# A trajectory blend with a routed expert network on one core: scales from sums of squares, a gate that carries the factor, one z operation, weights by chunk

## The chip, the cores and the metric

The kernel runs on one core of a Trainium2 chip. The metric is the time of one execution on the device, in microseconds; the kernel before has a median of 218.2 us over three runs (217.67 to 218.41). All work is one launch; five engines (TensorE, VectorE, ScalarE, GpSimd, and SyncE, which starts transfers) run their own instruction lists and wait for each other by semaphores.

## What is computed

The input is 16 sequences of 256 tokens with 128 features (4096 tokens). First a guided trajectory over a window of eight differences is added and normalized; then each token goes through one of eight experts, chosen by the router, and is normalized again.

```python
diffs = x[:, 1:] - x[:, :-1];  windows = the last 8 diffs at each position
mag = norm(windows);  normed = windows / mag;  combined = pos_weights * tanh(2 * mag)
g_weights = softmax(2 * cos(normed, guidance));  influence = g_weights @ guidance
traj = sum((0.6 * normed + 0.4 * influence) * combined) / sum(combined)
x = layernorm(x + traj)                                     # x1
logits = x @ Wr + br;  gates = max(softmax(logits));  e = argmax(logits)
xn = layernorm(x) * ln_g + ln_b
h = relu(xn @ W1[e] + b1[e]);  y = (h @ W2[e] + b2[e]) * gates      # 128 -> 512 -> 128
x = layernorm(x + y)
```

## The kernel before

**Stage 1** handles the tokens in eight parts (index u) of 512 tokens, as four tiles of 128. It is pipelined by hand: an outer iteration i, from -2 to 11, holds on each engine the pieces of several parts, in a fixed order. On VectorE it is `window(i)` (L706: the step v = i - 1 that makes V from the influence, the step y = i - 2 that makes Y = x + traj and its statistics, the routing steps r = i - 3 and g = i - 4, all interleaved with `drain`s), then `diff(i + 2)` (the differences Dd), `factors` (reciprocal magnitudes of part i + 1, the bias term of x1 of part i - 2), and `directions(i + 1)` (the normalized N). On ScalarE it is nT (copy of the transposed N), weights_hi from i = 7 on, ET (the exponential, L586), ex, tanh of part i + 1, x1 of part i - 2 (L593), four squares with sums of part i + 2 (L559), xT, V of part i + 1 (L573). On TensorE it is the transpose of N, logits of part i - 3 (L445), similarities of part i (L454), traj of part i - 1 (L433), rank of part i - 3, influence of part i (L406), transpose of x1 of part i - 2. On GpSimd it is the root of the squares (L340), the two roots of the variance (L345, L349) and, from i = 4, `scatter(i - 4)`: four indirect DMAs (L357) that write each token's row of 132 values (x1, gate, second root, token number) to a table in HBM sorted by expert.

**Scales.** TensorE multiplies in fp16 with weights and activations split into a high and a low part, each scaled by a power of two. The scales come from maxima of the absolute values: VectorE's `maxima1` (W1, L844, after `directions` in i = 0 and 1) and `maxima2` (W2, L849, and the small ones, before `directions` in i = 2 to 4), a transpose and a product on TensorE in i = 5, and ten `scales` steps in window 6. Then ScalarE writes the high parts of the weights (L611, L612, two experts at a time) in i = 7 to 10 and VectorE the low parts (L909, L911) in i = 7, in i = 9, and twice behind the table of blocks. The biases are split into three parts by ScalarE (L635, L638, L639) and VectorE (L901 in i = 8, L904 in i = 9).

**Between the stages** VectorE makes the table of blocks (which rows and which expert each of the 39 blocks of 128 rows has), SyncE waits for all scatters and TensorE for the low parts of the weights.

**Stage 2** runs over 39 blocks, again as a pipeline in a fixed order per engine, written with `steps([(lead, function), ...])`: in step b a function with lead d handles block b + d. SyncE loads a row tile XR (L303), eight buffers. ScalarE: xs (L649, lead 5), hh (L663, lead 1), OUT (L672, lead -3), xt (L654, lead 4), sd (L668, lead -2), xh (L658, lead 4). TensorE: h (L526 to L530, lead 1), the transpose of xs (L501, lead 4), the next eight expert numbers into registers (L511, every eighth step), y (L540 to L543, lead 0; hh times 256 columns of W2hl, which holds high and low part side by side, then hl times the high part). VectorE: hl (L986, lead 1), mv (L1005, lead -1), zpart (L991, lead 0), the reciprocal (L1009, lead -2), z (L995, lead 0), the shift (L1013, lead -2), bn (L999, lead 0), xl (L980, lead 4). GpSimd: the store of OUT by token number (L388, lead -3), then cg, the gate times the inverse scale, and a copy of the token number (L381, L382, lead 3).

Of the kernel before, what the change touches and what calls it, by code (L numbers as in the profile page):

```python
# [41 lines left out]
UN = 8  # L42
LN_EPS = 1e-5
# [37 lines left out]
def build(nc, x, guide, wr, br, ln_g, ln_b, w1, b1, w2, b2, cst, rows, out):  # L81
    with ExitStack() as ctx:
# [3 lines left out]
        def sem(name):  # L86
# [22 lines left out]
        W1h = sb("W1h", [P, E, FF], F16)  # L109
        W1l = sb("W1l", [P, E, FF], F16)  # L110
        W2hl = sb("W2hl", [P, E, FC, 2 * D], F16)
# [4 lines left out]
        mx = sb("mx", [P, 16])  # L116
        mx4 = sb("mx4", [4, 8])
# [49 lines left out]

        XR = [sb(f"XR{i}", [P, ROW]) for i in range(UN)]
        tok = [sb(f"tok{i}", [P, 1], I32) for i in range(UN)]
        xs = [sb(f"xs{i}", [P, D]) for i in range(UN)]  # L170
        cg = [sb(f"cg{i}", [P, 1]) for i in range(UN)]
# [5 lines left out]
        z0 = [sb(f"zpart{i}", [P, D]) for i in range(UN)]  # L177
# [3 lines left out]
        sd = [sb(f"sd{i}", [P, 3]) for i in range(UN)]  # L181
# [3 lines left out]
        ld = {n: sem("ld_" + n) for n in ("cst", "guide", "small", "x0", "x1", "x2", "x3", "w1", "w2", "bias")}  # L185
# [3 lines left out]
                 "counted guide_sq guide_norm guided guideT_ps guideT split_hi split_lo maxima maxT_ps max4 maxb_ps max_read scales_w "  # L189
# [5 lines left out]
        names2 = "xs xh xl hl z".split()  # L195
        t = {n: [sem(f"b_{n}{i}") for i in range(UN)] for n in names2}

        every = {n: sem("every_" + n) for n in "token xT_ps xt h_ps hh y_ps z0 bn mv sd rec shift out".split()}
        seen = sem("seen")
        row_loaded = [sem(f"row_loaded{i}") for i in range(UN)]  # L200
# [5 lines left out]
        infl_ps, traj_ps, xT_ps, log_ps = [bank[2], bank[3]], [bank[4], bank[5]], bank[6], bank[7]  # L206
        rank_ps = bank[5][:, 300:300 + NT * E]
# [13 lines left out]

        LO_AT = (7, 9)
# [28 lines left out]
        def _(sp):  # L251
# [14 lines left out]
            for n, (a, b) in enumerate(((2, 6), (6, 10), (10, 16)), 1):  # L266
                sp.dma_start(X[:, a:b, :, :], x[a:b].rearrange("b (p c) d -> p b c d", c=2)).then_inc(ld[f"x{n}"], 16)
                next_rows(a, b, f"x{n}")
                if n == 1:
                    sp.dma_start(W1[:, :, :], w1.rearrange("e d f -> d e f")).then_inc(ld["w1"], 16)  # L270
            sp.dma_start(Wr[:, :], wr).then_inc(ld["small"], 16)
            sp.dma_start(brb[:, :], br.rearrange("(a e) -> a e", a=1).to_broadcast([P, E])).then_inc(ld["small"], 16)
            sp.dma_start(gb[:, 0:1], ln_g.rearrange("(d a) -> d a", a=1)).then_inc(ld["small"], 16)
            sp.dma_start(gb[:, 1:2], ln_b.rearrange("(d a) -> d a", a=1)).then_inc(ld["small"], 16)
            sp.dma_start(W2[:, :, :, :], w2.rearrange("e (c p) d -> p e c d", p=P)).then_inc(ld["w2"], 16)
            sp.wait_ge(s["zeroed"], 1)
            for j in range(3):
                sp.dma_start(bias[32 * j:32 * j + E, 0:FF], b1).then_inc(ld["bias"], 16)
                sp.dma_start(bias[32 * j:32 * j + E, FF:FF + D], b2).then_inc(ld["bias"], 16)
# [20 lines left out]
            def load(count, k):  # L300
                after(sp, every["z0"], blocks(count(-1), k))
                after(sp, every["token"], blocks(count(-1), k))
                sp.dma_start(XR[k][:, :], rows[bass.ds(row[count(0) * UN + k], P), :]).then_inc(row_loaded[k], 16)  # L303

            load_rows(0)
            for b in range(NB):
                if b % UN == UN // 2 and b + UN // 2 < NB:
                    load_rows(b + UN // 2)
                load(lambda d, turn=b // UN: turn + d, b % UN)
# [4 lines left out]
        def _(pool):  # L314
# [4 lines left out]
            pool.memset(mx[:, :], 0.0)  # L319
# [31 lines left out]

            def scatter(u):
                pool.wait_ge(s["placed"], u + 1)
                pool.wait_ge(s["x1"], u + 1)
# [12 lines left out]
            for i in range(-1, NU + 4):  # L367
                if i + 1 < NU:
                    mag_roots(i + 1)
                if 2 <= i <= NU + 1:  # L370
# [4 lines left out]
            def token(count, k):  # L375
                pool.wait_ge(row_loaded[k], count(1) * 16)
                pool.nop().then_inc(seen, 1)
                after(pool, stored[k], count(0) * 16)
                pool.nop().then_inc(seen, 1)

                pool.tensor_scalar(cg[k][:, :], XR[k][:, D:D + 1], scl[:, 3:4], None, ALU.mult)  # L381
                pool.tensor_copy(tok[k][:, :], XR[k][:, D + 2:D + 3].bitcast(I32)).then_inc(every["token"], 1)  # L382

            def store(count, k):
                pool.wait_ge(every["token"], blocks(count(0), k))
                pool.wait_ge(every["out"], blocks(count(0), k))
                pool.nop().then_inc(seen, 1)
                pool.indirect_dma_start(  # L388
                    out=out[:, :], out_offset=bass.IndirectOffsetOnAxis(ap=tok[k][:, 0:1], axis=0),
                    in_=OUT[k][:, :], in_offset=None, bounds_check=T - 1, oob_is_err=False).then_inc(stored[k], 16)  # L390

            steps([(-3, store), (3, token)])

        @block.tensor
        def _(pe):
# [13 lines left out]
            def xT_(u):  # L409
# [3 lines left out]
                if u == 3:  # L413
                    pe.wait_ge(s["max_read"], 1)
# [22 lines left out]
            def logits(u):  # L437
                pe.wait_ge(s["xT_sb"], u + 1)
                if u == 0:
                    pe.wait_ge(s["guideT"], 1)  # L440
                    pe.wait_ge(ld["small"], 64)
                if u >= 1:
                    pe.wait_ge(s["shifted"], u)
                for k in range(NT):
# [22 lines left out]
            for i in range(0, NU + 3):  # L467
                if i == 5:

                    pe.wait_ge(s["maxima"], 1)  # L470
                    pe.wait_ge(s["xT_sb"], 3)
                    pe.transpose(xT_ps[0:4, 0:P], mx[:, 0:4], ident).then_inc(s["maxT_ps"], 1)
# [564 lines left out]
```

## Time and profile before

| | |
|---|---|
| median of three runs | 218.2 us (217.67 to 218.41) |
| the profiled execution | 218.13 us, span 216.3 us |
| mean granted TensorE clock | 0.811 of 2.4 GHz |
| busy: TensorE, VectorE, ScalarE, GpSimd | 150.0, 171.1, 141.6, 122.3 us |
| stage 1: first load to last scatter | 0.7 to 120.5 us |
| stage 2: first row load to last store's start | 123.0 to 209.3 us |

The profile page comes from one execution by the hardware profiler, times in microseconds from the start of the span. A row of a timeline gives start, duration, engine, line of the kernel, operation, output and inputs, and in brackets how long the engine stood idle before it and what released it; "issue" is time in which it waited for nothing that the profile shows. A duration includes the latency of the operation; neighbours on an engine overlap a little, so the distance from start to start is what an operation costs on a full engine. The granted clock is a share of 2.4 GHz: 0.50 is 1.2 GHz, 1.00 is 2.4 GHz. PE is TensorE, DVE VectorE, ACT ScalarE, POOL GpSimd, SP SyncE; PEld is the load of TensorE's stationary operand.

### The profile page before, as it was taken

How to read it: one execution, taken by the hardware profiler on the slowest of the kernel's cores; microseconds unless marked ns; L12 is line 12 of the kernel's file. 1: busy time of each engine (PE TensorE's matmuls, PEld its weight loads, DVE VectorE, ACT ScalarE, POOL GpSimd, SP SyncE). 2: the span in 40 equal slices, each digit the busy share in tenths (PEclk: the TensorE clock that was granted, in tenths of full speed). 3: DMA queues.
4: the chain of work that ended last, by engine and by line, in shares of the span. 5: the costliest groups of instructions: out<-in, count | busy, mean ns of one | idle time of the engine just before them, and what ended most of it. 6: DMA issues, size and time to landing. Idle time of an engine off the chain costs nothing.

```text
span 216.3 us, 5485 instructions
## 1 busy us (share of the span) xinstructions
PE 150.0 (69%) x1395; PEld 125.7 (58%) x1395; DVE 171.1 (79%) x792; ACT 141.6 (65%) x425; POOL 122.3 (57%) x210
## 2 busy tenths in 40 slices
PE   0057974998777898674510069999899999899600
PEld 0015753685756487573400059899798898788400
DVE  2447789878998988986868517999999999999910
ACT  2357627483835567737712078999999999998530
POOL 4322213423728775877877240377777787678670
PEclk9999997575888597855555558999999999999955
DMA  5996770000100100001015140222222222220000
GB/s 147 355 364 193 213 200 0 3 0 2 39 13 22 34 25 25 27 28 50 25 52 150 36 89 16 50 66 60 70 74 77 71 64 70 75 64 23 31 10 2
DMA packets 16417, 15.76 MB, mean 73 GB/s; under 512 B 2810, under 2 KB 13142, under 8 KB 16386
## 3 DMA queue, kind: packets, MB, share of 16 engines
q1 hardware_dynamic: 13458, 10.83, 18.3%
q0 software_dynamic: 2272, 4.27, 6.0%
q10 hardware_dynamic: 656, 0.30, 0.5%
q8 instruction: 13, 0.21, 0.4%
q14 instruction: 18, 0.15, 0.2%
HBM read 10.52 MB, written 5.33 MB: 73 GB/s over the span
## 4 chain that ended last, share of the span: by engine, by line
PE 21%; ACT 20%; POOL 18%; DVE 15%; issue 13%; DMA 5%; DVEq 2%; SPq 1%; ACTq 1%; POOLq 1%
POOL rows L357 12%; ACT OUT L672 4%; PE bank L433 3%; PE bank L540 3%; DMA XN<-in_attn_embeddings 3%; ACT xs L649 3%; DVE hl L986 3%; ACT xt L654 3%; PE bank L454 3%; POOL rstd L345 2%; POOL R L349 2%; ACT sq L559 2%; ACT hh L663 2%; PE bank L526 2%; PE bank L528 2%
## 5 line engine op out<-in xcount | busy, mean ns | idle before, releaser
L388 POOL DMA_INDIRECT out<-OUT,tok x39 | 40.4, 1037 | 25.1 <-issue 23.9
L357 POOL DMA_INDIRECT rows<-R,place x32 | 34.0, 1061 | 9.0 <-issue 9.0
L526 PE MATMUL bank<-sel,bias 96*128 96x128 bf16 x156 | 35.2, 226 | 0.0
L540 PE MATMUL bank<-W2hl,hh 128*128 x156 | 32.6, 274 | 3.5 <-issue 2.6
L528 PE MATMUL bank<-xh,W1h 128*128 128x128 f16 x156 | 34.9, 224 | 0.0
L530 PE MATMUL bank<-xh,W1l 128*128 128x128 f16 x156 | 34.7, 223 | 0.0
L529 PE MATMUL bank<-xl,W1h 128*128 128x128 f16 x156 | 34.7, 222 | 0.0
L433 PEld LDWEIGHTS bank<-V,C 128*128 128x128 f32 x128 | 24.9, 299 | 11.2 <-issue 11.2
L986 DVE SCALAR_TENSOR_TENSOR hl<-bank,hh 128x512 f16<-128x512 f32 x39 | 26.9, 690 | 3.0 <-ACT hh L663 2.8
L433 PE MATMUL bank<-V,C 128*128 128x129 f32 x128 | 26.8, 393 | 3.0 <-DVE Y L753 3.0
L543 PE MATMUL bank<-W2hl,hl 128*128 x156 | 27.9, 219 | 0.0
L663 ACT ACTIVATE hh<-bank 128x512 f16<-128x512 f32 x39 | 23.4, 599 | 3.2 <-PE bank L530 2.7
L501 PE MATMUL bank<-C,xs 128*128 128x128 f32 x39 | 11.7, 300 | 14.0 <-ACT xs L649 14.0
L672 ACT ACTIVATE OUT<-z,sd 128x128 f32<-128x128 f32 x39 | 19.6, 502 | 2.5 <-DVE sd L1013 2.5
L649 ACT ACTIVATE xs<-XR 128x128 f32<-128x128 f32 x39 | 15.9, 408 | 7.9 <-DMA XR<-rows 7.6
L540 PEld LDWEIGHTS bank<-W2hl,hh 128*128 128x128 f16 x156 | 15.2, 98 | 8.7 <-issue 7.0
L345 POOL TENSOR_TENSOR rstd<-var_in,minus_half 128x4 f32<-128x4 f32 x8 | 8.2, 1020 | 20.0 <-DVE var_in L784 20.0
L654 ACT ACTIVATE xt<-bank,gbs 128x128 f32<-128x128 f32 x39 | 18.0, 462 | 0.0
L454 PE MATMUL bank<-nT,gdT 128*64 128x512 f32 x16 | 13.1, 911 | 5.0 <-ACT nT L580 5.0
L381 POOL TENSOR_SCALAR cg<-XR,scl 128x1 f32<-128x1 f32 x39 | 12.0, 309 | 7.3 <-DMA XR<-rows 5.5
L528 PEld LDWEIGHTS bank<-xh,W1h 128*128 x156 | 15.8, 101 | 0.1
L526 PEld LDWEIGHTS bank<-sel,bias 96*128 96x128 bf16 x156 | 15.5, 99 | 0.4
(161 smaller groups left out, 448.9 us busy)
## 6 DMA issues: line engine op xcount, KB each, us to landing
XR<-rows SPq DMA_DIRECT2D x39, 66.0 KB, 2.0
W<-in_ffn_W SPq DMA_DIRECT2D x1, 2048.0 KB, 11.3
X<-in_attn_embeddings SPq DMA_DIRECT2D x2, 512.0 KB, 9.0
X<-in_attn_embeddings SPq DMA_DIRECT2D x1, 768.0 KB
out<-OUT,tok POOLq DMA_INDIRECT x39
XN<-in_attn_embeddings SPq DMA_DIRECT2D x2, 256.0 KB, 8.2
rows<-R,place POOLq DMA_INDIRECT x32, 2.4
C<-in_constants SPq DMA_DIRECT2D x1, 428.0 KB, 5.2
```

Of the source, the lines that this page charges most:

```text
L357: pool.indirect_dma_start(out=rows[:, :], out_offset=bass.IndirectOffsetOnAxis(ap=place[u % 4][:, k:k + 1], axis=0), in_=R[u % 4][:, k, :] ...
L388: pool.indirect_dma_start(out=out[:, :], out_offset=bass.IndirectOffsetOnAxis(ap=tok[k][:, 0:1], axis=0), in_=OUT[k][:, :], in_offset=None ...
L433: m = pe.matmul(tile_of(traj_ps, k), band[a][k % 2], V[u % 3][:, 2 * (k // 2) + a, :], start=a == 0, stop=a == 1)
L526: pe.matmul(h, bias3[:, c * P:(c + 1) * P], sel, start=True, stop=False)
L528: pe.matmul(h, wh, xh[k][:, :], start=False, stop=False)
L529: pe.matmul(h, wh, xl[k][:, :], start=False, stop=False)
L530: m = pe.matmul(h, wl, xh[k][:, :], start=False, stop=True)
L540: pe.matmul(y[:, 0:2 * D], hh[k][:, c * P:(c + 1) * P], w, start=c == 0, stop=False)
L543: m = pe.matmul(y[:, 0:D], hl[k][:, c * P:(c + 1) * P], wh, start=False, stop=c == FC - 1)
L663: act.activation(hh[k][:, :], bank[1 + k % 4][:, :], ACT.Relu).then_inc(every["hh"], 1)
L672: act.activation(OUT[k][:, :], z[k][:, :], ACT.Identity, scale=sd[k][:, 1:2], bias=sd[k][:, 2:3]).then_inc(every["out"], 1)
L986: stt(hl[k][:, :], bank[1 + k % 4][:, :], 0.0, hh[k][:, :], ALU.max, ALU.subtract).then_inc(t["hl"][k], 1)
```

## The change

Five parts.

1. The scales come from sums of squares in place of maxima. ScalarE squares W1 (i = 0, 1), the small tensors (i = 2) and W2 (i = 2, 3) with an accumulated sum, between nT and ET; one matmul on TensorE in i = 3, ahead of infl, sums over the partitions; the steps stand in window 4 (the last ones behind its last cast, each behind a drain), with one more root on GpSimd. The loads of the biases, the gains and W2 move ahead in SyncE's list.
2. The inverse of the scales is multiplied into the gate in stage 1 (`gated`, on VectorE, which the scatter waits for), so that stage 2 needs no cg; the store reads the token number from the row tile itself. Row tiles get 16 buffers, and a load of block b waits for the store of block b - 16.
3. y is accumulated in 128 columns, the low part of W2 added in the same place: one z operation.
4. The last scaling moves from ScalarE (OUT, lead -3) to VectorE (`b_fin`, lead -2), as (z - mean) * reciprocal; the shift goes.
5. The weights are split by chunks of 128 of the 512 middle features, in separate tiles; the high parts are written in i = 5 to 8, the bias parts in i = 5 to 7.

```diff
             for n, (a, b) in enumerate(((2, 6), (6, 10), (10, 16)), 1):
                 sp.dma_start(X[:, a:b, :, :], ...)
                 next_rows(a, b, f"x{n}")
                 if n == 1:
                     sp.dma_start(W1[:, :, :], w1.rearrange("e d f -> d e f")).then_inc(ld["w1"], 16)
+                    sp.wait_ge(s["zeroed"], 1)
+                    (six bias loads, two of the gains)
+                if n == 2:
+                    sp.dma_start(W2[:, :, :, :], w2.rearrange("e (c p) d -> p e c d", p=P)).then_inc(ld["w2"], 16)
...
-            steps([(-3, store), (3, token)])
+            steps([(0, store)])
...
+                if i == 3:
+                    pe.wait_ge(s["sums"], 6)
+                    pe.wait_ge(s["gains"], 1)
+                    pe.wait_ge(s["shifted"], 1)
+                    pe.matmul(sums_ps, ones[:, :], sums[:, :], start=True, stop=True).then_inc(s["sums_ps"], 1)
...
+                pe.matmul(y[:, 0:D], sel16[...], bias3[:, FF:FF + D], start=True, stop=False)
                 for c in range(FC):
-                    pe.matmul(y[:, 0:2 * D], hh[k][:, c * P:(c + 1) * P], w, start=c == 0, stop=False)
-                    m = pe.matmul(y[:, 0:D], hl[k][:, c * P:(c + 1) * P], wh, start=False, stop=c == FC - 1)
+                    pe.matmul(y[:, 0:D], hh[k][:, c * P:(c + 1) * P], wh, start=False, stop=False)
+                    pe.matmul(y[:, 0:D], hl[k][:, c * P:(c + 1) * P], wh, start=False, stop=False)
+                    m = pe.matmul(y[:, 0:D], hh[k][:, c * P:(c + 1) * P], wl, start=False, stop=c == FC - 1)
...
+            def squares_w1(q):
+                if q == 0:
+                    act.wait_ge(ld["w1"], 16)
+                act.activation(junk[:, :], W1[:, 2 * q:2 * q + 2, :], ACT.Square, accum_out=sums[:, 8 + q:9 + q])
+                act.drain()
...
                 if 0 <= i < NU:
                     nT_(i)
-                if i >= NU - 1:
-                    weights_hi(i - NU + 1)
+                if 0 <= i < 2:
+                    squares_w1(2 * i)
+                    squares_w1(2 * i + 1)
+                if i == 2:
+                    squares_bias()
+                if 2 <= i < 4:
+                    squares_w2(2 * i - 4)
+                    squares_w2(2 * i - 3)
+                if i in HI_AT:
+                    weights_hi(HI_AT.index(i))
                 if 0 <= i < NU:
                     et(i)
...
-            steps([(5, b_xs), (1, b_hh), (-3, b_fin), (4, b_xt), (-2, b_sd), (4, b_xh)])
+            steps([(5, b_xs), (1, b_hh), (4, b_xt), (-2, b_sd), (4, b_xh)])
...
+            def gated(g):
+                if g >= 4:
+                    dve.wait_ge(scattered[g % 4], 16 * NT * (g // 4))
+                ts(R[g % 4][:, :, D], gate[:, :], scl[:, 3:4], None, ALU.mult).then_inc(s["gated"], 1)
...
                     dve.tensor_copy(oh16[:, :, :], oh[:, :, :]).then_inc(s["onehot"], 1)
-                if i == 6:
-                    scales(9)
+                if i == 4:
+                    scales(6)
+                    for step in range(7, 11):
+                        dve.drain()
+                        scales(step)
+                    dve.drain()
+                    gated(0)
...
-                if 8 <= i <= 9:
-                    split_bias(i - 8)
+                if 6 <= i <= 7:
+                    split_bias(i - 6)
...
-            steps([(1, b_hl), (-1, b_mv), (0, b_z0), (-2, b_rec), (0, b_z), (-2, b_shift), (0, b_bn), (4, b_xl)])
+            steps([(1, b_hl), (-1, b_mv), (0, b_z), (-2, b_rec), (0, b_bn), (-2, b_fin), (4, b_xl)])
```

## Rows read from the trace of the kernel before

**Rows 1.** Chain of work that ended last: start, duration, what

```profile
119.57 2.34 DMA rows<-R,place
```

**Rows 2.** Timeline of GpSimd, a scatter of part 5

```profile
104.02 2.00 POOL L357 DMA_INDIRECT rows<-R,place  x1 [0.18 <-issue]
```

**Rows 3.** Timeline of VectorE in stage 1

```profile
46.70 0.24 DVE L727 RECIPROCAL st<-bank 128x2 f32<-128x2 f32 x2 [1.01 <-PE bank L406]
...
95.02 0.81 DVE L901 TENSOR_TENSOR bias_r<-bias 96x640 f32<-96x640 f32 x1
...
100.55 0.19 DVE L771 TENSOR_TENSOR lg<-bank,brb 128x32 f32<-128x32 f32 x1 [1.39 <-PE bank L445]
...
109.74 0.19 DVE L808 TENSOR_TENSOR oh<-oh,rt 128x32 f32<-128x32 f32 x1
110.00 0.18 DVE L813 CAST oh<-oh 128x32 bf16<-128x32 f32 x1
```

**Rows 4.** Busy time by stretch: PE, PEld, DVE, ACT, POOL, granted clock, DMA

```profile
42.00:44.00 2.00, 2.00 (x11) 2.00 (x11) 1.92 (x6) 1.25 (x6) 0.83 (x2) 0.50 0.04 8
...
150.00:170.00 20.00, 18.89 (x266) 17.14 (x265) 19.67 (x86) 19.75 (x64) 15.40 (x31) 1.00 0.26 70
```

**Rows 5.** Timeline of VectorE in stage 2

```profile
129.94 0.69 DVE L986 SCALAR_TENSOR_TENSOR hl<-bank,hh 128x512 f16<-128x512 f32 x1 [0.97 <-ACT hh L663]
...
166.35 0.69 DVE L986 SCALAR_TENSOR_TENSOR hl<-bank,hh 128x512 f16<-128x512 f32 x1
...
167.04 0.32 DVE L991 SCALAR_TENSOR_TENSOR zpart<-bank,cg,XR 128x128 f32<-128x128 f32 x1
167.28 0.15 DVE L1009 RECIPROCAL sd<-sd 128x1 f32<-128x1 f32 x1
...
167.66 0.15 DVE L1013 SCALAR_TENSOR_TENSOR sd<-mv,sd 128x1 f32<-128x1 f32 x1
167.78 0.29 DVE L999 BATCH_NORM_STATS2 bn<-z 128x6 f32<-128x128 f32 x1
...
168.24 0.69 DVE L986 SCALAR_TENSOR_TENSOR hl<-bank,hh 128x512 f16<-128x512 f32 x1
```

**Rows 6.** Timeline of TensorE in stage 2: transposes, and a y

```profile
132.77 0.28 PE L501 MATMUL bank<-C,xs 128*128 128x128 f32 x1
...
134.52 0.28 PE L501 MATMUL bank<-C,xs 128*128 128x128 f32 x1
...
185.22 0.28 PE L540 MATMUL bank<-W2hl,hh 128*128 x1 [0.91 <-issue]
```

**Rows 7.** Timeline at the end: last hl, last store

```profile
202.58 0.69 DVE L986 SCALAR_TENSOR_TENSOR hl<-bank,hh 128x512 f16<-128x512 f32 x1
...
209.25 0.97 POOL L388 DMA_INDIRECT out<-OUT,tok  x1 [0.30 <-issue]
```

**Rows 8.** Groups of instructions by line and shape: busy, mean ns, idle before

```profile
L672 ACT ACTIVATE OUT<-z,sd 128x128 f32<-128x128 f32 x39 | 19.6, 502 | 2.5 <-DVE sd L1013 2.5
...
L836 DVE TENSOR_SCALAR N<-Dd,st 128x128 f32<-128x128 f32 x32 | 7.1, 286 | 0.7
...
L559 ACT ACTIVATION_READ_ACCUMULATOR sq<-Dd 128x1 f32 x32 | 6.0, 187 | 0.0
...
L849 DVE TENSOR_REDUCE mx<-W 128x1 f32<-128x1024 f32 x4 | 4.8, 1210 | 0.0
...
L611 ACT ACTIVATE W1h<-W,scl 128x1024 f16<-128x1024 f32 x4 | 4.6, 1140 | 0.0
```

**Rows 9.** Timeline of ScalarE, the exponential of part 0

```profile
16.15 0.59 ACT L586 ACTIVATE ET<-bank 64x512 f32<-64x512 f32 x1 [2.06 <-PE bank L454]
```

**Rows 10.** Page, part 6, DMA issues: KB each, us to landing

```profile
W<-in_ffn_W SPq DMA_DIRECT2D x1, 2048.0 KB, 11.3
```

**Rows 11.** Timeline of TensorE in stage 1, traj of parts 1 and 2

```profile
29.95 2.02 PE L433 MATMUL bank<-V,C 128*128 128x129 f32 x16 [0.61 <-DVE Y L753]
...
41.41 3.81 PE L433 MATMUL bank<-V,C 128*128 128x129 f32 x16
```

More of the change, by code:

```diff
@@ L42 @@
 UN = 8
+RN = 16
 LN_EPS = 1e-5
@@ L193, in build @@
         padded = sem("padded")
-        names2 = "xs xh xl hl z".split()
+        names2 = "xs xh xl hl".split()
         t = {n: [sem(f"b_{n}{i}") for i in range(UN)] for n in names2}
-        every = {n: sem("every_" + n) for n in "token xT_ps xt h_ps hh y_ps z0 bn mv sd rec shift out".split()}
+        every = {n: sem("every_" + n) for n in "xT_ps xt h_ps hh y_ps z bn mv sd rec out".split()}
         seen = sem("seen")
-        row_loaded = [sem(f"row_loaded{i}") for i in range(UN)]
+        row_loaded = [sem(f"row_loaded{i}") for i in range(RN)]
         stored = [sem(f"stored{i}") for i in range(UN)]
@@ L298, in load_rows, with load @@
                     row[first + j] = sp.snap(held_row[half + j], min_val=0, max_val=PADROW)
[L300 to L303, printed above, removed]
+            def load(b):
+                if b >= RN:
+                    sp.wait_ge(stored[b % UN], 16 * ((b - RN) // UN + 1))
+                sp.dma_start(XR[b % RN][:, :], rows[bass.ds(row[b], P), :]).then_inc(row_loaded[b % RN], 16)
             load_rows(0)
@@ L467, in _ @@
             for i in range(0, NU + 3):
[L468 to L472, printed above, removed]
                 if i < NU:
@@ L478, in _ @@
                     sims(i)
-                if i == 5:
-                    pe.wait_ge(s["max4"], 1)
-                    pe.matmul(xT_ps[:, P:P + 4], ones[0:4, :], mx4[:, 0:4], start=True, stop=True).then_inc(s["maxb_ps"], 1)
                 if 1 <= i <= NU:
@@ L660, in b_hh @@
             def b_hh(count, k):
-                act.wait_ge(every["token"], blocks(count(0), k))
                 act.wait_ge(every["h_ps"], blocks(count(0), k))
@@ L665, in b_sd @@
             def b_sd(count, k):
-                after(act, stored[k], count(0) * 16)
                 act.wait_ge(every["mv"], blocks(count(0), k))
                 act.activation(sd[k][:, 0:1], mv2[k][:, 1:2], ACT.Sqrt, bias=epsc[:, 0:1]).then_inc(every["sd"], 1)
-            def b_fin(count, k):
-                act.wait_ge(every["shift"], blocks(count(0), k))
-                act.activation(OUT[k][:, :], z[k][:, :], ACT.Identity, scale=sd[k][:, 1:2], bias=sd[k][:, 2:3]).then_inc(every["out"], 1)
-            steps([(5, b_xs), (1, b_hh), (-3, b_fin), (4, b_xt), (-2, b_sd), (4, b_xh)])
+            steps([(5, b_xs), (1, b_hh), (4, b_xt), (-2, b_sd), (4, b_xh)])
         @block.vector
@@ L861, in power, with gain_sums @@
-            def power(dst, src, k, second):
-                if second:
-                    return ts(dst.bitcast(I32), dst.bitcast(I32), -1.0, float((254 + k) << 23), ALU.mult, ALU.add)
-                return ts(dst.bitcast(I32), src.bitcast(I32), POW2_MASK, None, ALU.bitwise_and)
+            def gain_sums():
+                dve.wait_ge(s["sums"], 4)
+                ts(sums[:, 0:4], sums[:, 8:12], sums[:, 13:14], None, ALU.mult).then_inc(s["gains"], 1)
+            QX, QH, Q2, Q1 = range(4)
```

243 lines of the change are left out of this document (114 added, 129 removed).

## The prediction, made before the changed kernel was run

> **What bounds the kernel now.** I read the busy times by stretch first, then the chain of work that ended last, then the timelines of single engines. The kernel has two stages with different limits. Stage 1 ends when the last scattered row has landed: the last landing begins at 119.57 us [rows 1], and only then are block rows fetched. That chain runs along GpSimd: twelve scatters, of parts 5, 6 and 7, follow each other without a wait from 104.02 us [rows 2], about 1.27 us from start to start. What set 104.02 is the root of part 7, which waits for VectorE's variance, which stands behind a wait of 1.39 us for the logits of part 6 [rows 3], which come through ScalarE and TensorE from the root of part 6. So before 104 us GpSimd, VectorE and ScalarE hand one chain around; what any of them adds there shifts the end.
> In stage 2, VectorE is busy 19.67 and ScalarE 19.75 of 20 us, TensorE 18.89 [rows 4]. VectorE starts hl every 1.89 us (166.35, 168.24) [rows 5]. TensorE needs less where it waits for nobody: 1.75 us from transpose to transpose (132.77, 134.52) [rows 6]. So VectorE and ScalarE bound a block and TensorE is 0.14 us behind them. From the first hl (129.94) [rows 5] to the last (202.58) [rows 7] there are 38 intervals in 72.64 us, 1.91 each.
>
> **Stage 2, part by part.** VectorE loses the first of two z operations: 0.24 us from its start to the next (167.04 to 167.28), and the shift, 0.12 (167.66 to 167.78) [rows 5]. It gains the last scaling, a tensor_scalar of 128x128 with two pointer scalars; its nearest row is L836, 0.286 us alone [rows 8], about 0.22 where four follow each other (my reading: 0.88 for four). 1.89 - 0.24 - 0.12 + 0.22 = 1.75, or 1.81 if the whole 0.286 shows. ScalarE loses OUT, 0.50 alone [rows 8], at least 0.38 between neighbours: about 1.50, free. GpSimd loses two small operations and keeps the store; it was not the bound. TensorE's y goes from four matmuls of 256 columns and five of 128 to thirteen of 128: the columns are the same, four more instructions cost about 0.01 in all: 1.76. So the bound passes to TensorE, with VectorE level with it.
> Now its stalls count. Every eight blocks the sequencer loads expert numbers and TensorE stands 0.6 to 1.1 us (0.91 at 185.22) [rows 6]; four such stalls. Before, VectorE didn't notice them. Behind a TensorE without slack each costs its whole length, about 0.75. Floor: 38 x 1.76 + 4 x 0.75 = 69.9; with some jitter between two equal engines 70.3. Against 72.64 that is 2.3 us less (bounds: 3.3 less if half of the stalls hide, 0.8 less if VectorE needs 1.81 and the stalls are not caught up).
> The fill of stage 2 is limited by landing rows and the first matmuls, which the change leaves: zero (if sixteen early fetches crowd the first four, up to +0.5).
> The end: last hl at 202.58, last store started at 209.25 [rows 7], 6.67 us. The stores of the last four blocks stand 1.27 apart on GpSimd. The scaling now comes one block earlier in the order than OUT did, so the last store is bound by GpSimd: the store of the fourth block from the end can start 1.6 us after the last hl, three more follow at 1.27, 5.4 us: 1.2 us less (0 to 2.0).
>
> **Stage 1, part by part.** Removed from VectorE: eight maxima of 1.21 us [rows 8], of which the four of W1 lay behind waits at 17 to 26 us, and some 1.2 us of smaller ones and waits; the scales of window 6, about 1.65 with the two bias scalings. Added to ScalarE: eight squares. The nearest row is L611, 1.14 us for the same shape, plus 0.187 for reading the accumulator [rows 8], less an overlap of 0.1 and plus a drain: 1.3 each, 2.6 per iteration, ahead of the exponentials (L586) of iterations 0 to 3.
> The Trainium skill (ScalarE: Activation LUTs, What ACT_TABLE_LOAD costs) gives 186 ns + 0.833 ns per element for an ACTIVATE with an immediate scale: 1.04 us for a square, by an estimate from that page. By that the two squares would be 0.2 us shorter; the sum keeps the row.
> Iteration 0: ScalarE waited 2.06 us for the similarities before L586 at 16.15 [rows 9]. W1 lands at about 14.1 to 14.6 (issued at 3.3, 11.3 to landing) [rows 10], so two squares end at 16.7 to 17.2 and L586 comes 0.6 to 1.05 late. Everything behind it on ScalarE (tanh, squares of the next part, V, nT) is on the chain there: +0.6 to +1.05 from then on. In iterations 1 to 3 the squares delay L586 by 1.6 to 3.4 us, which traj on TensorE mostly hides: it took 3.81 us at 41.41 [rows 11], at 1.2 GHz (granted 0.50 in that stretch) [rows 4]. The cover is thin: infl comes about 0.2 us later still, with the new matmul ahead of it, and VectorE waited for infl already (1.01 us at 46.70) [rows 3]. So window 4 starts its V about 1.2 to 1.6 us late, and the maxima removed from iterations 2 and 3 bring nothing, since what follows waits for TensorE.
> Iteration 4 holds the scales. Inside the window they add about 0.7; behind the last cast come gbs, four more steps and the gate's product, with drains. A drain with one small operation takes 0.26 (109.74 to 110.00) [rows 3]; five of these, the two bias scalings (0.75) and gbs make 2.4. So the differences of part 6 and the bias term of part 2's x1 come some 4.3 us late, while directions, in front of which 3.55 us of maxima vanish, come 0.8 late. ScalarE then runs x1, four squares, xT, V and nT of the next part in that order: nT of part 5 is 4 us late, similarities and traj follow, and infl of part 5 is 2 to 3 us late; VectorE had about 1.3 us before it needed that. At window 6 the delay is 1 to 2 us; its removed scales (1.65) bring it to about +0.5 at its end, but the split of the bias (0.81 at 95.02) [rows 3] moved there takes it back, and infl of part 6 (bias copy on ScalarE, 0.72, ahead of nT) holds window 7 at +1.5. In iteration 7 the second bias piece, 0.82, moves in front of window 8. Before, both stood where VectorE waited for logits anyway (the 1.39) [rows 3]. The root of part 6 is then 2.0 to 2.4 late, and that delay goes on to the last scatter one to one.
> Queues passed. SP: six bias and two gain loads stand ahead of x[6:10] and W2 ahead of x[10:16]; both were needed late (22 us and 42 us), some 7 MB have come by then at the 330 to 400 GB/s of the first slices: zero, at most +1. GpSimd: the root of the weights (1.02) waits for window 4's third step and lies under the wait for the variance of part 2; the first scatter, which waits for the gate, is 3.4 us late, behind it the root of part 6, but GpSimd stood idle 4.2 us before the next variance: absorbed. The weights' high parts move from iterations 7 to 10 to 5 to 8, under waits of ScalarE; the low parts stay, two of four behind the table, and end about 0.9 us before the rows land: hidden.
> Sum of stage 1: +1.9 (between -1.5, if TensorE runs at 2.4 GHz where it had 1.2 and the squares hide, and +4.5).
>
> **Sum.** The profiled execution has 218.13 us, of which 216.3 is span; 0.07 under the median of 218.2. 218.13 + 1.9 - 2.3 - 1.2 = 216.5.
>
> **A rule against the change.** In stage 1 one scatter took 2.00 us against 0.96, at 104.02 [rows 2], while VectorE split weights (two SBUF inputs). A store in stage 2 takes 1.05 and 0.36 of issue, 1.41 of 1.76. If the new scaling on VectorE held it as long as that scatter was held, GpSimd would need 2.4 per block and 38 blocks would take 91 us: 238. If it is held only for the 0.286 of the scaling, 1.69 stays under 1.76. The Trainium skill (Advanced Engine Details and Errata, VectorE Performance Modes) says that VectorE's second SBUF port is shared with GpSimd and that two-port instructions block it, which a fp32 tensor_scalar in SBUF can be; by that rule, the trace agrees for the splits.
>
> **The rivals.**
> A (the forecast, 0.42): stage 1 later by about 1.9, stage 2 shorter by 3.5.
> B, stage 1 doesn't shift (0.25): the squares hide fully and fewer stalls keep TensorE at 2.4 GHz, where traj takes 2.02 (29.95) instead of 3.81 [rows 11]. For it: VectorE loses some 6.8 us of work in iterations 2 to 5 and it is busy nearly throughout. Against: in iterations 3 and 4 TensorE's own work fills the period. 218.1 - 0.3 - 3.5 = 214.3.
> C, slower (0.19): the chain diff, x1, squares, xT, V, nT behind window 4 finds TensorE at 1.2 GHz, and the two bias splits add; similarities (1 us more) and traj (1.8 more) then lie on the path. It decides once infl of part 5 is more than 3.5 us late. Stage 1 +4.7, stage 2 -3.0: 219.8.
> D, no change (0.12): TensorE's stalls and VectorE at 1.81 leave 0.8 in stage 2, the end 0.9, stage 1 +1.9: 218.3.
> E, GpSimd becomes the bound of stage 2 (0.02): 238, above.
>
> **How the numbers follow.** About 0.3% (0.65 us) is what a measurement can tell from no change: faster is below 217.5, slower above 218.9. A lies mostly below 217.5 (0.34 of 0.42, the rest within), B below; C and E above; D within, a third of it above. Faster 0.59, same 0.16, slower 0.25. The likeliest time is A's 216.5. The range 213.2 to 220.2 takes in B and most of C; A's own range is 215.0 to 218.0.
>
> **What would show it.** Right: OUT is gone from ScalarE and it idles about 0.3 us per block; TensorE goes from transpose to transpose in 1.76 to 1.80; hl first to last about 70.3; last hl to last store 5.4; L586 of part 0 near 17 us; the last scatter starts near 121.5. Wrong: a last scatter before 119 (then B), after 123 (then C); hl intervals at 1.85 or more between the stalls; a store longer than 1.3 us; a ScalarE wait for W1 or W2.

## The result, and the profile after

The changed kernel takes 226.5 us (median of four runs, 226.04 to 226.72) against 218.3 us for the kernel before beside it (217.67 to 220.16): a ratio of 1.036, with a 95% interval of 1.029 to 1.042. The profiled execution took 226.56 us with a span of 224.3, against 218.13 and 216.3. So it is 8 us slower where 1.7 us faster was forecast, and outside the range of 213.2 to 220.2. Of the some 10 us between forecast and result, 7.7 arose in stage 2, 1.2 in stage 1 and 0.9 at the end.

The span divides at four points that both traces have. All times are us.

| | before | after | difference | forecast |
|---|---|---|---|---|
| last scatter starts | 119.57 | 122.66 | +3.1 | +1.9 |
| from there to the first hl | 10.37 | 10.23 | -0.1 | 0 |
| first to last hl, 38 intervals | 72.64 | 78.01 | +5.4 | -2.3 |
| last hl to last store | 6.67 | 6.35 | -0.3 | -1.2 |

The ends of these stretches in the trace of after, from the timelines of GpSimd and VectorE (start, duration, engine, line, operation, and in brackets how long the engine stood idle before it and what released it), to be held against [rows 2, 5, 7]:

```profile
122.66 0.96 POOL L368 DMA_INDIRECT rows<-R,place  x1 [0.30 <-issue]
...
132.89 0.69 DVE L992 SCALAR_TENSOR_TENSOR hl<-bank,hh 128x512 f16<-128x512 f32 x1 [0.91 <-ACT hh L697]
...
210.90 0.69 DVE L992 SCALAR_TENSOR_TENSOR hl<-bank,hh 128x512 f16<-128x512 f32 x1 [0.36 <-ACT hh L697]
...
217.25 0.98 POOL L393 DMA_INDIRECT out<-OUT,XR  x1 [0.31 <-issue]
```

Stage 2 is where most of it went. Busy times of after in 150 to 170 us (busy us and number of instructions of TensorE, its weight loads, VectorE, ScalarE, GpSimd; granted clock, DMA share, GB/s), the counterpart of [rows 4]:

```profile
150.00:170.00 20.00, 19.45 (x296) 17.93 (x296) 17.66 (x69) 15.74 (x50) 9.58 (x10) 1.00 0.23 59
```

VectorE has gone from 19.67 to 17.66 and ScalarE from 19.75 to 15.74, so both have the room that the change was to give them (a part of it only because the blocks are longer). What they wait for stands in the list of waits of after (us in total, times, longest):

```profile
POOL out L393 <- DVE OUT L1017: 53.7, 35, 17.6
ACT hh L697 <- PE bank L532: 19.2, 39, 1.7
DVE hl L992 <- ACT hh L697: 8.5, 25, 0.9
```

The shares of the chain that ended last, by engine, in the page of after (TensorE had 21% before):

```profile
PE 49%; ACT 12%; DVE 12%; DMA 7%; issue 7%; POOL 4%; DVEq 3%; ACTq 1%; SPq 1%; POOLq 1%
```

In stage 2 the waits lead to TensorE: GpSimd waits for VectorE, VectorE for ScalarE, ScalarE for TensorE, and from 140 to 200 us no wait of TensorE for one of them is listed. A piece of its timeline shows what it does in y:

```profile
162.94 0.22 PE L540 MATMUL bank<-bias,sel 96*128 96x128 bf16 x1
163.00 0.22 PE L543 MATMUL bank<-W2h,hh 128*128 x1
163.06 0.22 PE L544 MATMUL bank<-W2h,hl 128*128 x1
163.12 0.22 PE L545 MATMUL bank<-W2l,hh 128*128 x1
163.17 0.22 PE L543 MATMUL bank<-W2h,hh 128*128 x1
163.23 0.22 PE L544 MATMUL bank<-W2h,hl 128*128 x1
163.28 0.22 PE L545 MATMUL bank<-W2l,hh 128*128 x1
163.49 0.22 PE L543 MATMUL bank<-W2h,hh 128*128 x1
163.54 0.22 PE L544 MATMUL bank<-W2h,hl 128*128 x1
163.60 0.22 PE L545 MATMUL bank<-W2l,hh 128*128 x1
163.71 0.22 PE L543 MATMUL bank<-W2h,hh 128*128 x1
```

The matmuls follow each other in 0.05 to 0.06 us, but twice, ahead of L543, the next one starts 0.21 and 0.11 us after the matmul before it. A distance of 0.21 between starts is hidden by the 0.22 of duration, so no idle time is shown. From hl to hl it is 1.95 us now (median of the 38 intervals), 1.89 before. The instructions that stand in these places are not matmuls. The view of one line names them, with count, shortest, middle and longest duration in ns (PEldq is TensorE's sequencer). The high parts of y in after:

```profile
L543 PEldq ALU_OP  x156: 32/32/32, 133.6 to 212.4; - x156
```

The low parts of y in after, the same view:

```profile
L545 PEldq ALU_OP  x156: 32/32/32, 133.7 to 212.5; - x156
```

And y in the kernel before, the same view:

```profile
L540 PEldq FUSED_REGOPS  x156: 46/46/46, 130.7 to 203.8; - x156
```

Each different start of a weight slice that depends on the expert's number costs one computation of an address. The kernel before needs four per block in y, since the high part begins where the pair of both does; the changed one needs eight. h has eight in both. So a block has 12 before and 16 after.

The 32 ns of such a row are not what it costs. The starts of these rows in the trace of after show it: behind an ALU_OP the next address computation never begins sooner than 0.112 us, behind a FUSED_REGOPS never sooner than 0.124, with the matmuls and weight loads handed out in between. Without the pauses of more than 0.25 us they stand 0.120 apart on average. Sixteen of them make 1.92 of the 1.95 us of a block; twelve at that distance would make 1.44, less than the 1.75 that TensorE and VectorE need.

In stage 1 ScalarE does stand for W1, which was forecast as a sign of trouble:

```profile
15.44 1.06 ACT L613 ACTIVATE junk<-W 128x1024 bf16<-128x1024 f32 x1 [1.67 <-DMA W<-in_ffn_W]
16.40 0.18 ACT L613 ACTIVATION_READ_ACCUMULATOR junk<-W 128x1 f32 x1
16.66 1.06 ACT L613 ACTIVATE junk<-W 128x1024 bf16<-128x1024 f32 x1
17.62 0.19 ACT L613 ACTIVATION_READ_ACCUMULATOR junk<-W 128x1 f32 x1
17.90 0.59 ACT L588 ACTIVATE ET<-bank 64x512 f32<-64x512 f32 x1
```

The first exponential is 1.75 us late against [rows 9].

### The profile page after: what moved, and what is told of

Same layout as the page of the kernel before. It is cut to its first block, busy times and chain, and to the rows that moved or that the text cites. A ratio compares the mean times of both kernels' runs of the same rounds, so it can differ in the third digit from the quotient of the medians.

```text
span 224.3 us, 5683 instructions
## 1 busy us (share of the span) xinstructions
PE 153.5 (68%) x1550; PEld 129.1 (58%) x1550; DVE 158.7 (71%) x749; ACT 138.7 (62%) x405; POOL 104.6 (47%) x133
## 4 chain that ended last, share of the span: by engine, by line
PE 49%; ACT 12%; DVE 12%; DMA 7%; issue 7%; POOL 4%; DVEq 3%; ACTq 1%; SPq 1%; POOLq 1%
PE bank L543 6%; DMA W<-in_ffn_W 5%; PE bank L436 5%; PE bank L530 5%; PE bank L532 4%; PE bank L528 4%; PE bank L545 4%; PE bank L531 4%; PE bank L544 4%; PE bank L450 3%; POOL rows L368 3%; ACT R L595 3%; PE bank L459 3%; PE bank L503 2%; ACT sq L561 2%
## 5 line engine op out<-in xcount | busy, mean ns | idle before, releaser
L393 POOL DMA_INDIRECT out<-OUT,XR x39 | 38.3, 983 | 56.3 <-DVE OUT L1017 53.7
L545 PE MATMUL bank<-W2l,hh 128*128 x156 | 32.1, 218 | 0.0
L543 PE MATMUL bank<-W2h,hh 128*128 x156 | 31.8, 218 | 0.0
L544 PE MATMUL bank<-W2h,hl 128*128 x156 | 31.8, 218 | 0.0
L436 PEld LDWEIGHTS bank<-V,C 128*128 128x128 f32 x128 | 22.0, 267 | 10.5 <-issue 10.5
L436 PE MATMUL bank<-V,C 128*128 128x129 f32 x128 | 23.9, 361 | 1.5 <-DVE Y L785 1.5
L684 ACT ACTIVATE xs<-XR 128x128 f32<-128x128 f32 x39 | 15.3, 393 | 7.6 <-DMA XR<-rows 7.5
L689 ACT ACTIVATE xt<-bank,gbs 128x128 f32<-128x128 f32 x39 | 17.6, 452 | 0.1
L543 PEld LDWEIGHTS bank<-W2h,hh 128*128 128x128 f16 x156 | 15.1, 97 | 2.3
L532 PEld LDWEIGHTS bank<-xh,W1l 128*128 x156 | 15.3, 98 | 0.7
L531 PEld LDWEIGHTS bank<-xl,W1h 128*128 x156 | 15.6, 100 | 0.0
L528 PEld LDWEIGHTS bank<-sel,bias 96*128 96x128 bf16 x156 | 15.4, 99 | 0.0
```

What stands on the lines that cost most here:

```text
L393: pool.indirect_dma_start(out=out[:, :], out_offset=bass.IndirectOffsetOnAxis(ap=XR[b % RN][:, D + 2:D + 3].bitcast(I32), axis=0), in_=OUT ...
L436: m = pe.matmul(tile_of(traj_ps, k), band[a][k % 2], V[u % 3][:, 2 * (k // 2) + a, :], start=a == 0, stop=a == 1)
L528: pe.matmul(h, bias3[:, c * P:(c + 1) * P], sel, start=True, stop=False)
L531: pe.matmul(h, wh, xl[k][:, :], start=False, stop=False)
L532: m = pe.matmul(h, wl, xh[k][:, :], start=False, stop=True)
L543: pe.matmul(y[:, 0:D], hh[k][:, c * P:(c + 1) * P], wh, start=False, stop=False)
```

## The experiments

**Stage 2: what holds TensorE.** Theory Q: its queue can't deliver a block's matmuls, weight loads and address computations in 1.75 us. (The expectations call an address computation a register operation.) Four kernels were run together on one chip. In all four the trace shows something that neither kernel's had: 31 to 42 of some 176 signals of TensorE were seen 0.1 to 1.5 us after the matmul that sends them, also in stage 1, where three of the four kernels are the changed one but for the shape of a weight tile. One such place, from the timeline of wide_y (start, duration, engine, line, operation, idle time before it): TensorE's h ended at 153.50, and ScalarE, which waits for it alone, went on at 154.85.

```profile
153.28 0.22 PE L531 MATMUL bank<-xh,W1l 128*128 128x128 f16 x1
...
154.85 0.60 ACT L697 ACTIVATE hh<-bank 128x512 f16<-128x512 f32 x1 [1.44 <-PE bank L531]
```

Their times carry this, so I ran them again beside a control, on other chips. None of the other traces has one late signal in these bounds.

wide_y (y as before, z unchanged):

```diff
-                    pe.matmul(y[:, 0:D], hh..., wh, start=False, stop=False)
-                    pe.matmul(y[:, 0:D], hl..., wh, start=False, stop=False)
-                    m = pe.matmul(y[:, 0:D], hh..., wl, start=False, stop=c == FC - 1)
+                    w, wh = W2hl[c][:, bass.ds(e, 1), :], W2hl[c][:, bass.ds(e, 1), 0:D]
+                    pe.matmul(y[:, 0:2 * D], hh..., w, start=c == 0, stop=False)
+                    m = pe.matmul(y[:, 0:D], hl..., wh, start=False, stop=c == FC - 1)
```

> The changed kernel with TensorE's y as before (four matmuls of 256 columns, the low part of W2 beside the high one in each chunk's tile), VectorE's one z operation kept: it reads the first 128 columns, so the product of hh with the low part of W2 is left out of the result. Theory Q (TensorE's instruction queue can't deliver the instructions of a block in time: 30 matmuls with their weight loads and 16 register operations, 0.53 us of them; about 0.047 us per matmul and load): 26 matmuls and 12 register operations are 1.6 us, the queue is no bound, blocks return to 1.76 us between the expert loads, and the time is 218.5 to 219.5. Rival V (VectorE's operations or the row tiles' waits make the block 2.05 long, TensorE only follows): 226.

Measured 229.95 us, 1.052 of before [1.047, 1.057], with the late signals.

one_address (in y `wh = wl = W2h[c][:, bass.ds(e, 1), :]`):

> The changed kernel, with y's third matmul reading the high part of W2 again in place of the low one (so the low part is left out and the high one counted twice): the same 29 matmuls, but four register operations of 32 ns fewer per block. Theory Q: the queue needs 1.81 to 1.84 per block, 38 blocks gain 4 to 5 us: about 222. Rival N (the number of matmuls alone counts, register operations run beside them): 226.

Measured 229.05, with the late signals. fixed_expert (all slices `[:, 0:1, :]`, the weights of expert 0 for every block):

> The changed kernel with the weights of expert 0 for every block, so that no address is computed on TensorE (the choice of the expert's weights is left out; the numbers of the experts are still loaded). Theory Q: the queue needs 1.4 per block, TensorE's and VectorE's 1.75 are the bound: 217.5 to 219. Rival N (matmuls alone): 226.

Measured 227.42, with the late signals. before_narrow_y (for c > 0 the matmul of 256 columns is two of 128):

> The kernel before with three of its four matmuls of 256 columns in y cut into two of 128 (same columns, same results in the same places; three matmuls and three register operations more per block), nothing else changed. Theory Q: 29 matmuls and 15 register operations, 0.63 us of them, need 1.95 to 2.0 per block against 1.89: 221 to 223. Rival V (the block's length comes from VectorE or ScalarE): 218.3.

Measured 224.88. Taken alone, the first three would have thrown theory Q over. The control:

> The changed kernel itself, unchanged, as a control on the chip of this call: in the runs wide_y, one_address and fixed_expert the profile shows signals of TensorE that reached ScalarE 0.4 to 1.3 us after the matmul, in stage 1 too, where their instructions are those of the changed kernel. Theory C (that comes with the chip or its state): this run shows them too and is slower than the first runs of the changed kernel, 228 to 232. Rival K (it comes with the kernels): 226.5, and signals at most 0.03 us late.

Measured 226.87, 1.036 of before [1.028, 1.045], no late signals. The changed kernel is at its 226.5 here, and the repeats below have no late signals either, with the same instructions. So they belong to the chip or its state of the first four runs, and the rival that puts them on the kernels is out.

> The run wide_y again, beside the control (the product of hh with the low part of W2 is left out of the result). Theory Q (TensorE's instruction queue bounds the changed kernel's block): 5 to 7.5 us under after_again. Rival L (blocks shorter than about 1.9 us are not to be had for another reason): within 2 us of after_again or above it.

> The run fixed_expert again, beside the control (all blocks take the weights of expert 0, no address is computed). Theory Q: 5 to 8 us under after_again. Rival L: within 2 us of it or above.

Measured: wide_y_again 217.46, 9.4 us under the control; fixed_expert_again 216.10, 10.8 under it. Both speak for theory Q and against rival L, but both gain more than Q's range allowed (5 to 7.5, and 5 to 8). Neither is a usable kernel: wide_y_again leaves a product out, fixed_expert_again the choice of the expert. Starts of TensorE's transpose in wide_y_again, 1.75 and 1.74 apart:

```profile
149.74 0.28 PE L502 MATMUL bank<-C,xs 128*128 128x128 f32 x1
...
151.49 0.28 PE L502 MATMUL bank<-C,xs 128*128 128x128 f32 x1
...
153.23 0.28 PE L502 MATMUL bank<-C,xs 128*128 128x128 f32 x1
```

Which of the two differences counts, four matmuls or four addresses?

> The run one_address again, on another chip (y's third matmul reads the high part of W2 in place of the low one, which is left out; four register operations fewer per block, the same matmuls). In the control of the second call blocks follow each other in 1.95 us between the expert loads; with all 16 register operations gone 1.75. Theory Q (a matmul with its load costs the queue about 0.047 us, a register operation 0.032 to 0.046, and they add up): 1.82, stage 2 shorter by 5 to 6: 220.5 to 221.5. Rival N (the count of matmuls alone): 226.

Measured 217.73, 0.999 of before [0.996, 1.002]. With all 29 matmuls and four address computations fewer, the block is back at 1.75, and first to last hl takes 69.09 us. That is more than Q forecast (1.82 per block, 220.5 to 221.5 us): it took the 32 ns of a row for the whole cost. By the distances of 0.12 above, four computations fewer put the sequencer at 1.44, so another bound takes over. The count of matmuls doesn't make the 1.95; rival N is out. It is not nothing, though: the 29 matmuls and the transpose now start 0.055 to 0.06 us apart all through a block (0.115 behind the transpose), and that is 1.75. That this run reads one weight tile less in y is not the reason either, since fixed_expert_again reads all of them and has the same 1.75. Busy times of it in the same 20 us show VectorE full again:

```profile
150.00:170.00 20.00, 19.50 (x330) 19.03 (x328) 19.54 (x78) 17.98 (x57) 10.79 (x11) 1.00 0.28 75
```

The other direction, on the kernel before:

> The run before_narrow_y again, on another chip (the kernel before, three of y's four wide matmuls cut in two). Theory Q: 28 matmuls, a transpose and 15 register operations (0.63 us) make 2.0 per block against 1.89: 221.5 to 223.5. Rival V (VectorE and ScalarE set the block): 218.2.

Measured 223.69, 1.027 of before [1.023, 1.030]; the median interval between hl is 1.95 and the sum 77.91, as in the changed kernel. That is just above the forecast of 221.5 to 223.5. Stage 1 is untouched (last scatter at 119.60). So most of TensorE's part of the change (three of its four wide matmuls), put alone into the kernel before, makes it slower by some 5.7 us.

And the vector part alone, before_light:

```diff
-            steps([(1, b_hl), (-1, b_mv), (0, b_z0), (-2, b_rec), (0, b_z), (-2, b_shift), (0, b_bn), (4, b_xl)])
+            steps([(1, b_hl), (-1, b_mv), (0, b_z0), (-2, b_rec), (0, b_bn), (-2, b_fin), (4, b_xl)])
```

> The kernel before with the vector part of the change alone: one z operation (it reads the first 128 columns of y; the product of hh with the low part of W2 is left out of the result) and the last scaling on VectorE in place of ScalarE, no shift. TensorE, GpSimd, the row loads, the weights' tiles and stage 1 stay. Theory Q: blocks of 1.75 to 1.78 between the expert loads, stage 2 shorter by 2 to 2.5, the end by 0.3: 215 to 216. Rival L: 217.5 to 220.

Measured 214.92, 0.987 of before [0.979, 0.994], just under the forecast. First to last hl takes 69.70. But it leaves out a product, so it is no replacement.

| kernel | matmuls in h and y | addresses | median interval of hl | 38 intervals |
|---|---|---|---|---|
| before | 25 | 12 | 1.89 | 72.64 |
| after | 29 | 16 | 1.95 | 78.01 |
| before_narrow_y_again | 28 | 15 | 1.95 | 77.91 |
| one_address_again | 29 | 12 | 1.75 | 69.09 |
| wide_y_again | 25 | 12 | 1.74 | 69.25 |
| fixed_expert_again | 29 | 0 | 1.75 | 66.67 |

The last row has one thing more than its expectation says. The expert numbers are not loaded there: its trace has no instruction on the line of these loads, where the changed kernel has five (the view of that line, durations in ns):

```profile
L511 PEldq TENSOR_LOAD <-blk_e x5: 593/607/1069, 125.3 to 191.1; - x5
```

So fixed_expert_again drops sixteen addresses and four loads at once, and its long intervals are gone with the loads (at most 2.01, where wide_y_again has up to 2.72 and the changed kernel 3.29). It can't tell what a load costs beside no addresses. The other rows can: the four intervals behind the loads exceed the median by 0.8 to 1.3 us each in the changed kernel, and by 0.3 to 1.0 in one_address_again and wide_y_again, with twelve addresses.

**A version with the whole result.** light_alt keeps y and both z of before, takes the last scaling of every second block from ScalarE to GpSimd and the gate's factor from GpSimd to ScalarE, and has 16 row tiles:

> A kernel with the whole result: the kernel before with the row tiles in 16 buffers, the store's index read from the row tile, the gate's factor multiplied on ScalarE, and the last scaling of even blocks on GpSimd, of odd ones on ScalarE (with their shift); y and both z operations as before. Theory Q: TensorE's queue as before (1.73 at most), VectorE 1.83, ScalarE about 1.8, GpSimd about 1.5: blocks of 1.83, and the expert loads show in part: 215.5 to 217. Rival G (GpSimd's scaling is slow or is held up by VectorE and stores come late): 218 or more.

Measured 225.54, 1.035 of before [1.030, 1.041]: rival G. The median interval is 1.86 (72.43 for 38), but GpSimd falls behind, and the last store starts 14.66 us after the last hl. Its timeline at the end:

```profile
206.14 0.97 POOL L394 DMA_INDIRECT out<-OUT,XR  x1 [0.30 <-issue]
207.15 0.80 POOL L386 TENSOR_SCALAR OUT<-z,mv,sd 128x128 f32<-128x128 f32 x1
208.85 1.06 POOL L394 DMA_INDIRECT out<-OUT,XR  x1 [0.90 <-POOL OUT L386]
210.22 0.98 POOL L394 DMA_INDIRECT out<-OUT,XR  x1 [0.30 <-issue]
211.24 0.80 POOL L386 TENSOR_SCALAR OUT<-z,mv,sd 128x128 f32<-128x128 f32 x1
```

A scaling costs 0.80 on GpSimd, and its store another 0.90 until it starts: 4.1 us for two blocks, where two blocks of the kernel before take 3.8. I found no whole version that beats the kernel before.

**Stage 1: where 3.1 us come from.** First the three suspects together, all_three (the moved scale steps in words):

```diff
-                if 0 <= i < 2:
-                    squares_w1(2 * i)
-                    squares_w1(2 * i + 1)
+                if 1 <= i < 3:
+                    squares_w1(2 * i - 2)
+                    squares_w1(2 * i - 1)
...
-                if i == 4:
-                    scales(6)
-                    (scales 7 to 10 and gated(0), each behind a drain)
+                if i == 4:          # behind directions(i + 1)
+                    (scales 6 to 10 and gated(0), each behind a drain)
...
-                if 6 <= i <= 7:
-                    split_bias(i - 6)
+                if 8 <= i <= 9:
+                    split_bias(i - 8)
```

> The changed kernel with three of its moves in stage 1 taken back or put elsewhere: W1's squares in iterations 1 and 2 in place of 0 and 1 (W2's first two behind the exponential of iteration 2), the last five scale steps and the gate's product behind the directions of iteration 4 in place of ahead of the differences, the bias parts in iterations 7 to 9 as before. Theory P (these are what moved the last scatter by 3.1 us): the last scatter at 119.5 to 120.5, 223.5. Rival S (the squares as such, 9.9 us of ScalarE): last scatter at 122 to 123, 225.5 to 226.5.

Measured 225.31, last scatter at 120.55. The last scatter is at the edge of theory P's range, but the time isn't at its 223.5: first to last hl took 78.52 here. Then each alone:

> The changed kernel with W1's squares in iterations 1 and 2 in place of 0 and 1 and W2's first two and the small ones behind the exponential of iteration 2; nothing else moved. Theory W (the wait for W1's landing and two squares, 1.75 us at the first exponential, are handed on to the end): last scatter at 121.2 or earlier, 225.0. Rival H (they are hidden again by iteration 4, what counts comes behind): last scatter within 0.5 of the changed kernel's 122.7 to 123.9, 226 to 227.

> The changed kernel with the last five scale steps and the gate's product behind the directions of iteration 4 in place of ahead of the differences; nothing else moved. Theory T (the differences of part 6 and the x1 of part 2, 3.7 us late there, carry most of the delay): last scatter 1.5 to 2.5 earlier, 224.5. Rival H2 (the waits for TensorE that follow take it up anyway): within 0.5, 226 to 227.

> The changed kernel with the bias parts on ScalarE in iterations 7 and 8 and on VectorE in 8 and 9, as before; nothing else moved. Theory B (two pieces of 0.81 us on VectorE ahead of windows 7 and 8 lie on the chain): last scatter 0.8 to 1.6 earlier, 225.3. Rival H3 (they lie under waits): within 0.3, 226 to 227.

V stands for VectorE's first operation on V in a part, which waits for the influence.

| kernel | first exponential | V of part 5 | V of part 7 | last scatter | median us |
|---|---|---|---|---|---|
| before | 16.2 | 69.8 | 89.4 | 119.57 | 218.3 |
| after | 17.9 | 71.8 | 92.2 | 122.66 | 226.5 |
| after_again | 17.3 | 72.5 | 93.4 | 123.89 | 226.9 |
| squares_later | 16.3 | 72.8 | 93.3 | 123.78 | 225.7 |
| tail_moved | 17.9 | 70.0 | 92.0 | 122.51 | 227.3 |
| bias_later | 17.6 | 72.4 | 90.9 | 121.47 | 226.4 |
| all_three | 15.5 | 68.9 | 90.4 | 120.55 | 225.3 |

How far one profile can be trusted here is to be read from five kernels whose stage 1 is the changed one (but for the shape of a weight tile in wide_y_again): their last scatters start at 122.66, 123.89, 123.66 (wide_y_again), 123.26 (fixed_expert_again) and 121.31 (one_address_again). They spread over 2.6 us, so a single difference smaller than that says little. (Five kernels with the stage 1 of before have 119.16 to 120.21. The two groups don't overlap, so stage 1 did become later.) By that squares_later moves nothing that one can see (H). Nor does tail_moved at the end (H2), though it brings the V of part 5 forward by 1.8 to 2.5 us against the two runs of the changed kernel, and by 1.0 against the earliest of the five; that is lost again by part 7. bias_later lies at the edge of the band (V of part 7 at 90.9 and the last scatter at 121.47, where one_address_again has 90.8 and 121.31). Only all three together leave the band, by 0.8 us. No total time is lower than the changed kernel's beyond the intervals; tail_moved, 1.046 of before [1.043, 1.049], is if anything slower. So no single cause of the 3.1 us was found; that the three moves together make most of them is suggested, not shown, and which share the bias pieces have stays open.

## Why the prediction was wrong, step by step

- **What bounds the kernel before: right.** The relief on VectorE and ScalarE alone gave 1.3% (before_light), 69.70 us for 38 intervals where I had 70.3 with the whole change. It leaves out a product of y as well, but that product's matmuls are still made.
- **VectorE's block at 1.75: right.** The median interval is 1.74 to 1.75 in one_address_again, wide_y_again, fixed_expert_again and before_light. TensorE needs as much with 29 matmuls, so they are level, as I had them.
- **"The columns are the same, four more instructions cost about 0.01 in all: 1.76": this step failed.** It costed matmuls by their columns and left out what the sequencer does between them. The cost was not in the four matmuls, which leave the block at 1.75 (one_address_again), but in four addresses that are easy to overlook in the diff: `wh` and `w` began at one address, `W2h[c]` and `W2l[c]` don't. Size: 1.95 us per block instead of 1.76, and 78.01 for the 38 intervals against 69.09 in one_address_again, 8.9 us. It stood in the trace of before, as a row of the sequencer on each line with `bass.ds(e, 1)`; I had looked at lines and engines, where sequencer rows aren't busy time. I had also taken 1.75 of TensorE [rows 6] for its floor under any list of instructions, while it was the floor of that list.
- **The expert loads: right in kind, with one reading wrong.** Four intervals from hl to hl over 2.2 us remain in after (2.76, 2.81, 2.91, 3.29: 0.8 to 1.3 over 1.95), and they count in full; I had 0.75 each. But "before, VectorE didn't notice them" is false: the kernel before has 2.17, 2.25, 2.01 and 2.48 in these places, over a median of 1.89. So a part of the four stalls was in the 72.64 already.
- **The end: -0.3 where -1.2 was forecast.** The last four stores are 1.28 apart as said. The first of them I let start 1.6 after the last hl. The scaling it waits for does start at 212.16, 1.26 after, and ends at 212.49, but the store starts 0.90 later, at 213.39; that distance I had left out. It stood in the trace of before too: the scaling of the fourth block from the end ended at 204.58 there, and its store started 0.86 later, at 205.44.
- **The fill: right,** 4.96 from first xs to first hl against 5.02 before, with sixteen early fetches.
- **Stage 1: +3.1 where +1.9 was forecast,** inside its bounds (-1.5 to +4.5), but in part by luck, since some of the steps were wrong. W1 landed at 15.4, not at 14.1 to 14.6, so the first exponential was 1.75 late and not 0.6 to 1.05. But that everything behind it is on the chain from then on is not borne out: the V of part 2 starts at 36.3 in both kernels (at 36.4 to 38.0 in the other four profiles of the changed stage 1), and squares_later gains nothing. The delay behind window 4 is there (the V of part 5 is 2.0 late), but it is not handed on one to one: the V of part 6 is 0.9 late, that of part 7 2.7.
- **Rival E and the shared port: out.** A store of after takes 0.98 us with VectorE's new scaling beside it and 0.98 without (1.04 in the kernel before). By the Trainium skill (Advanced Engine Details and Errata, VectorE Performance Modes) the two share a port; the trace agrees only on VectorE's side: in before_light its scaling takes 0.33 alone (two of 39) and 0.42 on average where it overlaps a store, up to 0.63; in after 0.33 alone and 0.36 with a store, up to 0.56.
- **The square's cost:** 1.06 us in the rows above, where I took 1.14 from a scaling of the same shape. The estimate from the Trainium skill (ScalarE: Activation LUTs, What ACT_TABLE_LOAD costs: 186 ns + 0.833 ns per element) was 1.04, and the trace agrees with it better than with my row.
- **The rivals:** C forecast slower, by stage 1 at 1.2 GHz (219.8). The kernel is slower, but in stage 2 it expected 3.0 us less, and no rival had the mechanism that made the kernel slower: a new bound on an engine that I had at 0.14 us of slack.

## What to carry to other kernels

Where an engine's slices depend on a register, count the addresses, not only the matmuls: each slice that begins elsewhere costs a computation in the sequencer (0.11 us or more until the next one could start here), and splitting a tile can double them. When a change relieves the bounding engines, list every row of the next one, sequencer rows too, before calling its present pace a floor. And time the kernel itself beside its variants: without that, three variants pointed the wrong way, with 11 to 13 us too much.

## What the runs showed of the hardware

- An address computation on TensorE's sequencer is a row of 32 ns (ALU_OP) or 46 ns (FUSED_REGOPS), but the next one starts no sooner than 0.112 or 0.124 us behind it (after, before). Sixteen in a block go with 1.95 us, fifteen with 1.95 (11 of them FUSED_REGOPS), twelve with 1.74 to 1.75.
- Nine matmuls in y, four of them of 256 columns, and thirteen of 128 columns with their weight loads both fit into a block of 1.74 to 1.75 (wide_y_again, one_address_again). A matmul of 128 columns with its weight load follows the one before it in 0.055 to 0.06 us at 2.4 GHz.
- A load of eight expert numbers into registers takes 0.6 to 1.1 us on the sequencer, and the interval behind it is longer by 0.8 to 1.3 us with sixteen addresses in a block and by 0.3 to 1.0 with twelve.
- On one chip signals from TensorE were seen 0.1 to 1.5 us late in four kernels; three of them took 11 to 13 us longer than on other chips, the fourth 1.2, and the kernel before, beside them, 218.7. Why is open.
- A tensor_scalar of 128x128 in fp32 takes 0.80 us on GpSimd (light_alt) and 0.33 on VectorE (after). From the end of the scaling to the start of the store that reads its tile, GpSimd takes at least 0.86 us in the kernel before and 0.90 in after.
